# Two heads in the two row halves of TensorE, and maxima over 1024 keys at once, in the two unmasked attention layers

## The reference

```
scores = q @ k.T / sqrt(8)          # 1024 x 1024
attn   = softmax(scores)            # over the keys, with the row maximum taken off
o      = attn @ v
```

## Time and profile before

| | us |
|---|---|
| median of 3 runs | 3079.77 |
| lowest, highest | 3077.18, 3091.7 |
| the profiled execution | 3072.83 |
| its span | 3071.0 |

### The profile page before, as it was taken

The page is one execution under the profiler, slowest core; times in us unless marked ns, Lnnn a source line. Parts: engine busy times, 40 slices in busy tenths (PEclk is TensorE's granted clock), DMA queues, the critical chain, the costliest instruction groups (busy, mean ns, idle before and its releaser), DMA issues.

```text
span 3071.0 us, 46683 instructions
## 1 busy us (share of the span) xinstructions
PE 2664.3 (87%) x16310; PEld 1124.2 (37%) x16310; DVE 2139.2 (70%) x4997; ACT 1791.6 (58%) x3615; POOL 704.7 (23%) x1297
## 2 busy tenths in 40 slices
PE   2568999989988988988999999989989999999955
PEld 1322333323423423544444444433335334334324
DVE  7567887878788776556656566688875885786710
ACT  1145776656756765544555555466767666766731
POOL 4011123413322321331112111011122222213222
PEclk9589999999999999999999999999999999999977
DMA  2321002211311321322111121111013104103113
GB/s 65 115 68 53 30 25 84 61 59 51 94 38 48 109 85 57 96 65 92 44 58 46 45 74 44 34 46 42 29 52 117 41 29 129 50 23 123 51 33 117
DMA packets 138267, 193.72 MB, mean 63 GB/s; under 512 B 20929, under 2 KB 89409, under 8 KB 137409
## 3 DMA queue, kind: packets, MB, share of 16 engines
q1 hardware_dynamic: 119632, 129.84, 13.4%
q0 software_dynamic: 17536, 59.58, 6.4%
q10 hardware_dynamic: 864, 1.30, 0.1%
HBM read 145.44 MB, written 47.97 MB: 63 GB/s over the span
## 4 chain that ended last, share of the span: by engine, by line
PE 39%; DVE 5%; DMA 3%; ACT 3%; POOL 2%; issue 2%; SPq 1%; POOLq 0%; DVEq 0%; ACTq 0%
PE bank L808 11%; PE bank L767 9%; PE bank L790 8%; PE bank L792 3%; DVE small L1133 3%; PE bank L879 2%; PE bank L869 2%; DMA WX<-in_experts,WI 1%; POOL x_sorted L1367 1%; ACT PB L966 1%; PE bank L818 1%; PE bank L794 1%; PE bank L770 1%; PE bank L686 1%; DVE W L1055 1%
## 5 line engine op out<-in xcount | busy, mean ns | idle before, releaser
L1133 DVE TENSOR_REDUCE small<-bank 128x1 f32<-128x512 f32 (+2 forms) x2816 | 1715.6, 646 | 590.3 <-PE bank L767 489.7
L966 ACT ACTIVATE PB<-bank 128x512 f32<-128x512 f32 (+2 forms) x2816 | 1459.4, 570 | 814.5 <-PE bank L790 478.9
L767 PE MATMUL bank<-RK 128*128 128x512 bf16 (+2 forms) x2816 | 1052.1, 375 | 202.6 <-DVE small L1133 89.9
L790 PE MATMUL bank<-RK 128*128 128x512 bf16 (+2 forms) x2816 | 1034.6, 369 | 18.3 <-ACT PB L966 13.9
L808 PE MATMUL bank<-PB,VP 128*32 128x512 f32 (+3 forms) x5632 | 775.1, 583 | 0.1
L767 PEld LDWEIGHTS bank<-RK 128*128 128x128 bf16 x2816 | 275.6, 98 | 923.5 <-issue 384.5
L1340 POOL CAST small<-small 128x8 bf16<-128x8 f32 x192 | 39.2, 204 | 1421.1 <-DVE small L1137 1409.7
L790 PEld LDWEIGHTS bank<-RK 128*128 128x128 bf16 x2816 | 276.8, 99 | 208.3 <-ACT PB L966 37.6
L792 PE MATMUL bank<-RK 128*128 128x512 bf16 (+3 forms) x768 | 252.0, 328 | 0.0
L808 PEld LDWEIGHTS bank<-PB,VP 128*32 128x32 f32 x5632 | 126.0, 109 | 299.4 <-issue 288.7
L1330 POOL MEMSET RK<- 3x1024 bf16 x170 | 161.0, 947 | 238.8 <-PE bank L790 226.6
(11 more groups left out here) (157 smaller groups left out, 1886.7 us busy)
## 6 DMA issues: line engine op xcount, KB each, us to landing
RK<-q_parts SPq DMA_DIRECT2D x512, 48.0 KB
RK<-k_parts SPq DMA_DIRECT2D x512, 48.0 KB
q_parts<-SC SPq DMA_DIRECT2D x120, 128.0 KB, 1.8
k_parts<-SC SPq DMA_DIRECT2D x88, 128.0 KB, 1.8
RK<-rq_parts SPq DMA_DIRECT2D x48, 192.0 KB
RK<-rk_parts SPq DMA_DIRECT2D x48, 192.0 KB
XSB<-x_sorted SPq DMA_DIRECT2D x40, 192.0 KB, 4.4
y_sorted<-XSB SPq DMA_DIRECT2D x40, 192.0 KB, 4.1
```

The costliest lines, as they stand in the source:

```text
L767: p = e.matmul(bank[k][:, 0:wd], slot(L, u, 0)[:, 128 * qt:128 * qt + 128], slot(L, u, 1)[:, 512 * kh:512 * kh + wd], start=True, stop=not ...
L790: p = e.matmul(bank[k][:, c0:512], slot(L, u, 1)[:, ks], slot(L, u, 0)[:, qs], start=True, stop=not ly.causal)
L966: e.activation(prob(L, t)[:, c0:512], bank[k][:, c0:512], ACT.Exp, scale=ly.scale).then_inc(bank_free[k], 1)
L1133: e.tensor_reduce(small[:, u % 2, 2 * qt + kh:2 * qt + kh + 1], bank[k][:, 0:wd], AX.X, ALU.max).then_inc(bank_free[k], 1)
```

## The change

Layers 0 and 2 (unmasked):

- six products of parts instead of nine (the three smallest left out), so a head fills 48 rows; with three rows of maxima 51. An even unit lies in rows 0 to 63 of `RK`, an odd one in rows 64 to 127, so there are 16 slots in the same space, and matmuls name only their 48 or 51 rows. Probability tiles of a pair come as two tiles of the odd unit, then two of the even one; maxima come as even unit, odd unit. In the order the two kinds alternate, so that neighbours stand in different row halves.
- no clearing of the rows of maxima (the maximum matmuls don't read them), two fetch DMAs of a unit instead of six, and six stored copies of q's and k's parts instead of five and three.

All layers:

- maxima of 128 queries over all their keys are one step in a two-bank tensor (`unit0` = banks 4 and 5, `unit1` = banks 6 and 7, in turn): two matmuls of up to 512 keys, one reduction over up to 1024, which also negates. `max_end` goes.
- the step of the list is now `score`: half a T pair, that is two `main` tiles and one maximum unit (in the causal layer four units in three steps). Maxima run 24 steps (48 tiles) ahead of the probabilities.
- `main` tiles, `send`, `turn` and all other work share banks 0, 1, 2 in turn; bank 3 is for `av`. A bank that other work has filled but not emptied is left out of the turn (`held`).
- the output steps of a pair (`out_rate`, four `out_head`) are one step, and the rotary products take one bank at a time.

The core of the diff:

```diff
@@ class Layer
-            self.mains = [(kt, hh, qh, 0) for kt in range(8) for hh in range(2) for qh in range(2)]
-            self.maxes = [(qt, kh, 512) for qt in range(8) for kh in range(2)]
-            self.q_seq, self.k_seq = ((0, 3), (1, 4), (2,)), ((0,), (1,), (2,))
-            self.slots, self.shift, self.lead, self.scale = 8, 2 * number, 12, 1.0 / float(np.sqrt(8.0))
+            self.mains = [(kt, hh, qh, 0) for kt in range(8) for hh in (1, 0) for qh in range(2)]
+            self.q_seq, self.k_seq = ((0, 3, 5), (1, 4), (2,)), ((0, 1, 2), (3, 4), (5,))
+            self.slots, self.scale = 16, 1.0 / float(np.sqrt(8.0))
@@ order_of_work
-    for T in range(LAYERS[2].t_main + LAYERS[2].tiles + 20):
-        P.base = 0 if T < LAYERS[0].lead else 3
-        if work and (T % 2 == 0 or T % 4 == 1 and 0 < T - LAYERS[1].t_main < 224):
-            one_step()
...
-            if 0 <= T - ly.t_max < ly.tiles:
-                P.do("max", L, T - ly.t_max, banks=(P.misc(3),))
-            g = T - ly.t_main
-            if 0 <= g < ly.tiles:
-                P.do("main", L, g, banks=(P.bank(T % 3),))
+    P.base, first_done = 0, pair_end[0, 31]
+    for h in range(-LEAD, len(halves) + 8):
+        for _ in range(2 if h < 0 or h % 2 and first_done < h < pair_end[1, 7] else 1):
+            if work:
                 one_step()
...
+            mains = [(t + i, P.misc()) for i in range(2)]
...
+        for a in take[h + LEAD] if h < len(halves) else ():
+            k = 4 + 2 * (P.count("unit", 1) % 2)
+            max_bank[a] = P.bank(k)
+            us.append((a, max_bank[a]))
+        if mains or us:
+            P.do("score", h, L=L, mains=mains, units=us)
+        if h >= 3 and h % 2 == 1 and h < len(halves) + 2:
...
+            P.do("av", L, gg, banks=(P.bank(3) if gg % per == 0 else P.step_of["av", L, gg - 1].banks[0],),
@@ slot
+            s, r = LAYERS[L].slot(u), 0
+            o = 2048 * s + 512 * k
+            if not LAYERS[L].causal:
+                o, r = 4096 + 1024 * (s // 2) + 512 * k, 64 * (s % 2)
+            return RK[r + r0:r + r1, o:o + 512].bitcast(BF16)
@@ tensor
+            def main(L, t, use):
...
+                if kt == 0:
+                    g.wait_ge(sent_sem[u % 4], step_of["send", L, u].more["total"])
+                g.wait_ge(bank_free[k], n - 1)
...
+                    p = e.matmul(bank[k][:, :], slot(L, u, 1, 0, 51)[:, ks], slot(L, u, 0, 0, 51)[:, qs], start=True, stop=True)
+            def maximum(v, i, use):
...
+                if i == 0:
+                    g.wait_ge(bank_free[k + 1], P.uses[k + 1])
+                    g.wait_ge(bank_free[k], n - 1)
...
+                p = e.matmul(unit[k // 2 - 2][:, c0:c1], slot(L, u, 0, 0, rows)[:, 128 * qt:128 * qt + 128],
+                             slot(L, u, 1, 0, rows)[:, c0:c1], start=True, stop=not diag)
...
+                elif kind == "score":
+                    for i in range(2):
+                        if s.a[0] % 2 == 0:
+                            for t, use in s.more["mains"][i:i + 1]:
+                                main(s.more["L"], t, use)
+                            for v, use in s.more["units"]:
+                                maximum(v, i, use)
+                        else:
+                            for v, use in s.more["units"]:
+                                maximum(v, i, use)
+                            for t, use in s.more["mains"][i:i + 1]:
+                                main(s.more["L"], t, use)
@@ vector
-                    e.tensor_reduce(small[:, u % 2, 2 * qt + kh:2 * qt + kh + 1], bank[k][:, 0:wd], AX.X, ALU.max).then_inc(bank_free[k], 1)
+                        e.tensor_reduce(small[:, u % 4, qt:qt + 1], unit[k // 2 - 2][:, 0:128 * (qt + 1) if LAYERS[L].causal else 1024],
+                                        AX.X, ALU.max, negate=True).then_inc(bank_free[k], 1)
@@ sync
-                        for i in range(3):
-                            e.dma_start(slot(L, u, 0, 24 * i, 24 * i + 24), QD[b, i:i + 3, rows, :]).then_inc(slot_sem[t], 16)
-                            e.dma_start(slot(L, u, 1, 24 * i, 24 * i + 24), KD[b, 0:3, rows, :]).then_inc(slot_sem[t], 16)
+                        e.dma_start(slot(L, u, 0, 0, 48), QD[b, :, rows, :]).then_inc(slot_sem[t], 16)
+                        e.dma_start(slot(L, u, 1, 0, 48), KD[b, :, rows, :]).then_inc(slot_sem[t], 16)
```

More of the change, by code:

```diff
@@ L180, in ssm_in, with next_scratch, parts @@
         yield from turned("s2", b)
[L183 to L196 removed]
+    def next_scratch():
+        mo["scratch"] = 1 - mo["scratch"]
+        return mo["scratch"]
+    def parts(kind, L, b, c, which, rows, copies, s):
+        scratch_user[s] = ((b, s, P.count(("parts", b, s), 16 * copies)),)
         P.do(kind + "_parts", L, b, c, which, slot=s, rows=rows)
[L198 removed]
     def qkv(L, b):
@@ L386, in finish @@
             one_step()
-    def fill(L, s, before):
-        if LAYERS[L].causal or s % 2 == 0:
-            P.do("fill", L, s, before=before, total=P.count(("fill", s), 16))
     def fetch(L, u):
@@ L423, in head_out @@
                 finish(("qkv", L + 1, b - 2) if b >= 2 else ("qkv", L, b + 2))
[L424 to L441 removed]
+        P.held.discard(P.step_of["turn", L, pr].banks[0][0])
@@ new lines, in heads_out @@
+        P.do("out_heads", L, pr, banks=P.step_of["turn", L, pr].banks)
+    units = [(ly.number, u + hh, qt) for ly in LAYERS for u in range(0, UNITS, 2) for qt in range(8) for hh in range(2)]
+    halves = [(ly.number, t) for ly in LAYERS for t in range(0, ly.tiles, 2)]
+    thirds, take = 0, []
+    for h in range(-LEAD, len(halves)):
+        n = -(thirds // 3)
+        thirds += 4 if h >= 0 and LAYERS[halves[h][0]].causal else 3
+        n += thirds // 3
+        take.append(units[thirds // 3 - n:thirds // 3])
```

379 lines of the change are left out of this document (167 added, 212 removed).

## The result

The changed kernel takes 3254.3 us (median of 4 runs, 3249.1 to 3267.5) where the kernel before took 3079.3 in the same session. The ratio is 1.057 with a 95% interval of 1.052 to 1.061: slower by 175 us, and forecast were 2850. The profiled execution has a span of 3251.6 us against 3071.0.

What follows compares the result with a forecast made beforehand. PE was taken to bound all three attention layers. Clean beats -185, hidden other work -95, shape changes +30 and shared banks +30 sum to -220 us, from 3072.8 to 2853; forecast 2850 us, own range 2780 to 2920, with rivals 2690 to 3020.

Steps and rivals of the forecast that it cites:

- Clean beat: Layers 0 and 2: a beat of four probability tiles goes from 2.83 to 2.46 us, 500 beats, -185 us.
- The chain of the fourth tile's bank: In each beat the fourth probability matmul needs the first one's bank; this loop of 2.46 us is the longest.
- the price of 0.86 us for eight scores: Score matmuls in layers 0 and 2: full overlap of row halves, 4 x 0.216 us, making PE's beat 1.97 us.
- Rival 3: Score runs of layers 0 and 2: PE changes shape and does not overlap, beat stays 2.83 us; 3170 us, 9%.
- A maximum over 1024 columns: DVE's reduction over two banks: 1.15 us each, 2.31 us a beat, bounds 1.15 and 1.24.
- Shared banks, +30 us: Layers 0 and 2: 301 probability matmuls take a bank last used by other work, 0.1 us each; at worst 346 us.
- rival 2: Shared banks cost half the worst case, 173 us in place of 30, and the clock slips: 2990 us, 15%.
- Layer 1, 0 us with bounds of -20 and +40: Causal layer keeps 128-row matmuls with PE 93% busy: no change; the upper bound is for the three shared banks.
- Other PE work half hidden, -95 us: Layers 0 and 2: 195 groups of other matmuls fall into PE's 0.49 us hole in mid-beat.
- the changes of shape, +30: PE in layers 0 and 2: 603 more changes of matmul shape at 0.05 us, range 0 to 60 us.
- DVE's smaller parts, fetches, clearing: 0: Dropped DVE work, fewer memsets on POOL and fewer fetch DMAs lie in slack or are hidden: 0 us.
- PE below 80% in layers 0 and 2: Sign that the forecast is right: PE busy below 80% in layers 0 and 2.

Runs made afterwards that it cites:

- e2: Changed kernel with the output's reader on DVE one step earlier, ahead of the maximum that stood before it: 3085.96 us, ratio 1.001.
- e1: Changed kernel with both heads of a neighbouring pair of score matmuls in the same row half: 3578.8 us, ratio 1.161.
- e10: Changed kernel with both probability tiles of a step ahead of its maxima in layer 1 alone: 3178.2 us, ratio 1.036.
- e6: e2 with both probability tiles of a step ahead of its maxima in layer 1: 2987.2 us, ratio 0.971.
- e11: e5 with both repairs, the early output step and layer 1's probability tiles ahead of the maxima: 3101.3 us, ratio 1.009.
- e4: Kernel before with only the row halves in layers 0 and 2, keeping its one-bank maxima and old order: 3031.0 us, ratio 0.982.
- e8: e4 with banks 3, 4, 5 and 7 in turn for maxima, everything else on banks 0 to 2: 2987.6 us, ratio 0.971.
- e5: Changed kernel with scores over 128 rows again (nine products, 8 slots, the clearing of before): 3249.9 us, ratio 1.058.

## Why the prediction was wrong

- **Clean beat.** 2.46 us forecast, 2.45 measured, with pairs that start together. The chain of the fourth tile's bank, and the price of 0.86 us for eight scores, were right. Rival 3 (no overlap) fell with this. What didn't come is 500 such beats: most had a wait or other work in them.
- **A maximum over 1024 columns.** 1.15 us each forecast; the timeline has two in 2.36 us, 1.18 each, and the mean duration of one is 1220 ns:

```profile
L1148 DVE TENSOR_REDUCE small<-unit 128x1 f32<-128x1024 f32 x1088 | 1300.9, 1220 | 543.3 <-PE unit L710 446.9 <-remote 45.1 <-PE unit L713 29.8
```

  Shapes xcount, busy us, mean ns, idle before it. Right.
- **Shared banks, +30 us: the step that failed.** The text had the mechanism ("at worst it waits behind one maximum of 1.15 us, 346 us" and "DVE and ACT both run dry") and took 0.1 us for each, by the nearest waits of the kernel before. Those were waits for readers that stood between maxima of 0.6 us. There was one misreading more: the earlier trace rows have 16 waits for a reader on ACT in 26.2 us, so a wait, where there is one, lasted 1.6 us before, too. The changed kernel's L688 waits for L1160 alone 82 us in 48 times, 1.7 us each, more than the worst that I allowed: ahead of L1160 stands not only the maximum's 1.23 us but DVE's own wait for PE ahead of it (0.82), and L1156 and L1160 themselves take 0.74 more. I had counted the instruction in front and not what that instruction waits for. e2 shows the size: 168 us for this one reader in place of 30 for all, of which half is waiting.
- **The granted clock, not a term of the sum at all.** It was named inside rival 2 ("a little may be lost there"). Layers 0 and 2 ran at 0.89 in place of 0.98 and 0.99. The one wait of 1.82 us that is shown above is followed by a beat of 3.62 us in place of 2.45, so it cost 1.2 us more than it lasted. And matmuls of half the rows are more exposed: e1 was on the slow clock at 100% busy.
- **Late starts beside POOL's DMA issues, not a term either.** The kernel before had none, so nothing in its rows could tell of them. In layers 0 and 2 the changed kernel spends 59 us more than e10 at these places, on top of what e2 repairs. Why it has them is open.
- **Layer 1, 0 us with bounds of -20 and +40.** It took +94. The shared banks were in the bounds; that a maximum has two buffers in place of three banks and more, and stands in front of probability tiles in PE's queue, was not. Putting the tiles first gave 37 us of it (e6 against e2; alone only 11, e10); the output reader accounts for about 21 (923 to 902), and 36 remain above the 829 of before, also with 128 rows in all layers (e11: 860; e4 and e8, with the old order: 833).
- **Other PE work half hidden, -95 us, and the changes of shape, +30.** Neither can be read off alone. Both together with the clean beat were to give -250. With both repairs e6 and e11 differ by 114, and e6 stands 137 above the forecast. That remainder is open: PE's matmuls still wait 95 us for a maximum's buffer (L710 for L1155), and the clock is 0.935 on the mean; in layer 2 it is 1.00 from 2080 to 2180 us, where little else runs, and 0.92 from 2680 to 2780, where much does.
- **DVE's smaller parts, fetches, clearing: 0.** No run speaks against it, and none tests it alone: e5 brings the clearing and the fetches back together with the 128 rows.
- **Reading PE's busy share.** I expected PE below 80% in layers 0 and 2. It reads 83%, and in the clean stretch of e2 below 97%, with holes that add up to half a microsecond in each beat (2.45 less 1.97): the modelled end of a matmul (0.39 us for a step of 0.22) fills them. A busy PE was no evidence either way.

The clean stretch of e2 (layer 2), columns as above:

```profile
2440.00:2460.00 20.00, 19.38 (x133) 4.55 (x131) 18.65 (x17) 16.65 (x34) 1.57 (x8) 1.00 0.07 22
```

Of the rivals, rival 2 (the banks bite and the clock slips) was the right mechanism at the wrong price: 2990 with half the worst case. That e6 and e8 end near 2990 is chance: they are other kernels. At the full worst case plus layer 1's bound the prediction's own numbers reach 3072.8 - 185 - 95 + 30 + 346 + 40 = 3209, far outside of the range of 2690 to 3020 that was given. The price of an unseen wait was taken near its lower bound, and the range with it.

## What to carry to other kernels

Before banks are pooled, write down for each reader what stands ahead of it on its engine and what that in turn waits for; if it waits for the engine that wants the bank, the wait is the whole loop, and moving the reader by one place can be worth more than the change itself. Price a wait of TensorE with the slow stretch behind it, not only with its own length. When a change in two parts loses, run each part alone on the old kernel: here one was worth 1.8% by itself, and 2.9% with other banks for the maxima. And when a kernel gains where nothing was edited, set both traces side by side, tile by tile, before crediting the edit: here some 60 us came and went at a dozen places.

## What was not expected of the hardware

- Score matmuls of 48 and 51 rows one after the other ran at a granted clock of 0.51 in a window with PE busy for 20.00 of 20 us, 0.853 over the whole of e1; 128-row ones in the changed kernel's order (e5) had 1.00 and 0.957. In pairs that overlap, half-row ones had 1.00 (e2's clean stretch). Of the two levels, 1.2 and 2.4 GHz, 0.51 is nearly all the lower one.
- A maximum over 1024 columns, across the border of two banks, takes 1220 ns, less than two of 682.
- Row halves overlap fully: starts within 10 ns, the next pair 0.23 us later, against 0.22 for one matmul alone.
- Beside trains of indirect DMA issues on POOL a result of PE reached DVE 2.2 us late and ACT stood idle for 2.86 us at the same time (e2, 444 us), in five of the kernels and not in the others with the same trains. What decides is open.
